# Window attention on one core: the row scores' stationary operand cut from 128 to 100 columns, and the odd half of the result combined in one instruction

## The chip, the cores and the metric

The kernel runs on one core of a Trainium2 chip. The metric is the device time of one execution in microseconds (us). A core has five engines with a queue of instructions each: TensorE (PE in the profile; its weight loads are listed apart as PEld), VectorE (DVE), ScalarE (ACT), GpSimd (POOL) and SyncE (SP), which issues the DMAs here. They work side by side and wait for each other through semaphores. TensorE's clock has two levels, 1.2 and 2.4 GHz; the profile gives the granted clock as a share of the upper one.

## The reference

The input `x` is 4 images of 128 channels and 112x112 pixels. It is group-normalised, goes through a windowed self-attention, and is added to the result:

```python
xs = jnp.roll(x, (-SHIFT, -SHIFT), axis=(-2, -1))            # SHIFT = 3
qkv = jnp.einsum('bchw,oc->bohw', xs, w_qkv) + b_qkv[None, :, None, None]
# 7x7 windows: 49 tokens each; 8 heads of 16 channels
scores = jnp.einsum('bxyhqd,bxyhkd->bxyhqk', q, k) * scale
attn = jax.nn.softmax(scores, axis=-1)
out = jnp.einsum('bxyhqk,bxyhkd->bxyhqd', attn, v)
# windows put back in place, rolled back
x = x + _L0_conv_ref(_gn(x), L0_conv_w_qkv, L0_conv_b_qkv)
```

## The kernel before

There are 4 x 16 x 16 windows of 49 tokens. The unit of work is a group of 8 windows (half a band of windows), so there are 128 groups. A group of 392 tokens goes through a software pipeline that is some four groups deep: in one step every engine works at different stages of groups g-3 to g+2, in an order that is written out by hand in a `step` function of each engine. Two steps stand in the body of a loop on each engine, and only semaphores tie the engines together.

TensorE's step is: `sum_keys` and `weigh` of group g-2, `project_v` of g, `turn_max` and `column_scores` (half 0) of g-1, `row_scores` (half 0) of g, `spread_inverse` of g-2, `project_k` of g+1, `column_scores` (half 1) of g-1, `row_scores` (half 1) of g, `project_q` of g+1. Products in which precision matters are computed with operands split into a high and a low float16 part, three matmuls for one product.

Heads come in pairs. Each pair has 32 channels, so it lies on a strip of 32 partitions, and the four strips hold the eight heads. `q_masks` holds, for each window, 100 columns: 49 queries and a zero with the channels of the even head kept, then 49 queries and a zero with those of the odd head kept. The scores are made twice. `row_scores` (L730) has queries on the partitions and keys along the columns, and exists only so that VectorE can take the maximum over the keys (`maximum`, L573). `column_scores` (L747, L756) has keys on the partitions, in two blocks of 64 rows for two windows, and feeds the exponential.

In `row_scores` the stationary operand is `q_masks[rows, ...]`, 32 partitions by 128 columns from the start of a window's 100, so that 28 columns of the next window (or of padding) are computed and never read; the moving operand is 49 columns of `k_hi` or `k_lo`. Each call makes 8 windows x 3 products x 2 head pairs, 48 matmuls. The two head pairs of a product stand on different strips of 32 partitions and write different banks, so they run side by side: a call is 24 such pairs of matmuls, each matmul with its own weight load. There are two calls in a group, 256 in all, and 12288 matmuls. `maximum` already reads only `psum[0:ROWS2]`, with ROWS2 = 100.

`weigh` (L794) multiplies the values by the probabilities into the two `OUT_BANKS`, one bank for each of the two windows of a pair of windows, at columns `a*100` for pair a of 4. Of each 100 columns, 49 belong to the even and 49 (from column 50) to the odd head. `evac_even` on ScalarE (L390) scales the even part into `even_out`, `join` on VectorE (L592) adds the scaled odd part, with one instruction for each bank, into `summed`, whose windows stand in their own order. `spread_inverse` (L806) spreads the inverse sums of the softmax, one matmul of 49 columns for each window, and `scale_rows` (L599) multiplies them with `summed` into `mixed`, which GpSimd adds to the image (L305).

Of the kernel before, what the change touches and what calls it, by code (L numbers as in the profile page):

```python
# [6 lines left out]
B, C, H, W = 4, 128, 112, 112  # L7
# [4 lines left out]
TOK = WS * WS  # L12
BANDS = H // WS
NW = W // WS
GW = NW // 2
GT = GW * TOK
HP = HEADS // 2
PC = 2 * HD
QP = TOK + 1
ROWS2 = 2 * QP  # L20
PITCH = 64
PAIRS = GW // 2
# [13 lines left out]
def window_attention(nc, x, w_qkv, b_qkv, out):  # L36
    f32, f16, bf16, i32 = mybir.dt.float32, mybir.dt.float16, mybir.dt.bfloat16, mybir.dt.int32
    ALU, ACT, AX = mybir.AluOpType, mybir.ActivationFunctionType, mybir.AxisListType
# [5 lines left out]
    with ctx:  # L44
        def sb(name, shape, dt=f32):
            return ctx.enter_context(nc.sbuf_tensor(name, shape, dt))

        def sem(name):
            return ctx.enter_context(nc.semaphore(name))
# [7 lines left out]
        q_masks = sb("q_masks", [C, 2, 2 * Q_LEN + Q_PAD], f16)  # L57
# [6 lines left out]
        inv_hi, inv_rows = sb("inv_hi", [C, TOK], f16), sb("inv_rows", [C, TOK], f16)  # L64
        even_out = sb("even_out", [C, 2, PAIRS, TOK])
        summed = sb("summed", [C, GW, TOK])
        mixed = sb("mixed", [C, 2, GW, TOK])
# [17 lines left out]
        pick_head = sb("pick_head", [C, GW, C], f16)  # L85
# [7 lines left out]
        v_scale = sb("v_scale", [C, 2])  # L93
# [11 lines left out]
        psum = ctx.enter_context(nc.psum_tensor("psum", [128, 8, 512], f32))  # L105
        ROW_BANKS, COL_BANKS, OUT_BANKS = slice(0, 2), slice(2, 4), slice(6, 8)
        NEG_BANK, SUM_BANK, QK_BANK, V_BANK, INV_BANK = 0, 3, 4, 5, 5
        SPARE_SUM = slice(PAIRS * ROWS2, PAIRS * ROWS2 + TOK)
        SPARE = slice(PAIRS * ROWS2, (PAIRS + 1) * ROWS2)

# [21 lines left out]
        even_done, join_done, mixed_done, add_done = (sem(n) for n in ("even_done", "join_done", "mixed_done", "add_done"))  # L132

        def wait(engine, semaphore, count):

            if not isinstance(count, int) or count > 0:
                engine.wait_ge(semaphore, count)  # L140
# [188 lines left out]
        def _(act):  # L329
# [56 lines left out]
            def evac_even(g):  # L386
                act.wait_ge(out_mm, g + 1)
                wait(act, join_done, g + 1)
                even = psum[:, OUT_BANKS, 0:PAIRS * ROWS2].rearrange("p s (a e q) -> p s a e q", e=2, q=QP)[:, :, :, 0, 0:TOK]
                nc.scalar.activation(even_out[:, :, :, :], even, ACT.Identity, scale=v_scale[:, 0:1]).then_inc(even_done, 1)  # L390

            def step(g, n, par):
                if live(g):
                    evac_q(g)
                if live(g + 2):
                    normalise(g + 2, n + 1, par)
                if live(g - 2):
                    evac_even(g - 2)
                    high_inverse(g - 2)
                if live(g - 1):  # L400
                    evac_neg(g - 1)
                if live(g):
                    evac_v(g, par)
                if live(g - 1):
                    exp(g - 1, 0)
                if live(g + 1):
                    evac_k(g + 1)
                if live(g - 1):
                    exp(g - 1, 1)
# [18 lines left out]
        def _(dve):  # L428
# [147 lines left out]
            def invert(g):  # L576
                dve.wait_ge(sum_mm, g + 1)
                nc.vector.reciprocal(inv32[:, :], psum[:, SUM_BANK, SPARE_SUM]).then_inc(inv_done, 1)

# [6 lines left out]
            def join(g):  # L586
                dve.wait_ge(even_done, g + 1)
                wait(dve, mixed_done, g + 1)
                by_side = summed[:, :, :].rearrange("p (a s) q -> p s a q", s=2)
                for s in range(2):  # L590
                    odd = psum[:, OUT_BANKS.start + s, 0:PAIRS * ROWS2].rearrange("p (a e q) -> p a e q", e=2, q=QP)[:, :, 1, 0:TOK]
                    last = nc.vector.scalar_tensor_tensor(by_side[:, s], odd, v_scale[:, 1:2], even_out[:, s, :, :], ALU.mult, ALU.add)  # L592
                last.then_inc(join_done, 1)

            def scale_rows(g, par):
                dve.wait_ge(inv_mm, g + 1)
                dve.wait_ge(join_done, g + 2)
                wait(dve, add_done, g - 1)
                nc.vector.tensor_tensor(mixed[:, par, :, :].rearrange("p w q -> p (w q)"), psum[:, INV_BANK, 0:GT],  # L599
                                        summed[:, :, :].rearrange("p w q -> p (w q)"), ALU.mult).then_inc(mixed_done, 1)  # L600

            def step(g, n, par, chunks=(), image_at=None, first=None, before=None, after=None):


                if first:
                    first()
                if live(g):
                    low_q(g)
                if live(g - 2):
                    invert(g - 2)  # L610
                if live(g):
                    mask_q(g, par)
                if live(g - 2):
                    low_inverse(g - 2)
                    join(g - 2)
                if before:
                    before()
                if live(g):
                    maximum(g, par, 0)
                for chunk in chunks:  # L620
                    take_stats(image_at + chunk * STAT, chunk)
                if after:
                    after()
                if live(g - 2):
                    scale_rows(g - 2, par)
                if live(g):
                    maximum(g, par, 1)
# [50 lines left out]
        def _(pe):  # L678
# [3 lines left out]
            for j in range(3):  # L682
                last = nc.tensor.transpose(psum[:, QK_BANK, j * C:(j + 1) * C], w_nat[:, j, :], ident[:, :])
# [36 lines left out]
            def row_scores(g, par, j):  # L720

                if j == 0:
                    pe.wait_ge(q_masked, g + 1)
                    pe.wait_ge(k_split, g + 1)
                wait(pe, max_done[1 - j], g + j)
                for w in range(GW):
                    for n, (low, k) in enumerate(((0, k_hi), (0, k_lo), (Q_LEN, k_hi))):
                        for h in (2 * j, 2 * j + 1):
                            rows = slice(h * PC, (h + 1) * PC)
                            last = nc.tensor.matmul(psum[:, ROW_BANKS.start + h - 2 * j, w * TOK:(w + 1) * TOK],  # L730
                                                    q_masks[rows, par, low + w * ROWS2:low + w * ROWS2 + 128], k[rows, par, w, 0:TOK],
                                                    start=n == 0, stop=n == 2, skip_group_check=True)
                last.then_inc(row_mm[j], 1)

# [39 lines left out]
            def sum_keys(g):  # L774
                pe.wait_ge(exp_done[0], g + 1)
                pe.wait_ge(exp_done[1], g + 1)
                for a in range(PAIRS):
                    for e in range(2):
                        for c in range(HP):
                            last = nc.tensor.matmul(psum[c * PC:(c + 1) * PC, SUM_BANK, SPARE_SUM],  # L780
                                                    sum_rows[:, a, e, :, :, :].rearrange("p t w s -> p (t w s)"),
# [4 lines left out]
            def weigh(g, par):  # L786
                pe.wait_ge(v_evac, g + 1)
                wait(pe, join_done, g + 1)
                pe.sem_inc(waited_pe, 1)
                for a in range(PAIRS):  # L790
                    for c in range(HP):
                        for s in range(2):
                            side = slice(PITCH * s, PITCH * (s + 1))
                            last = nc.tensor.matmul(psum[c * PC:(c + 1) * PC, OUT_BANKS.start + s, a * ROWS2:(a + 1) * ROWS2],  # L794
                                                    v_rows[side, par, a, c * PC:(c + 1) * PC], probs_t[side, c, a, :],
                                                    start=True, stop=True, skip_group_check=True)
                last.then_inc(out_mm, 1)

            def spread_inverse(g, after_v=True):
                pe.wait_ge(inv_split, g + 1)  # L800
                if after_v:
                    pe.wait_ge(v_evac, g + 3)
                else:
                    pe.wait_ge(mixed_done, g + 1)
                for w in range(GW):
                    last = nc.tensor.matmul(psum[:, INV_BANK, w * TOK:(w + 1) * TOK], pick_head[:, w, :], inv_rows[:, :],  # L806
                                            start=True, stop=True, skip_group_check=True)
                last.then_inc(inv_mm, 1)

# [51 lines left out]
```

## Time and profile before

| | |
|---|---|
| time, median of 3 runs | 1022.41 us (1020.85 to 1024.33) |
| the profiled execution's own time | 1024.01 us |
| its span, first to last instruction | 1022.1 us |
| mean granted clock of TensorE | 0.985 |
| matmuls and weight loads | 46595 each |
| of them row scores (L730) | 12288 each |

The span is the stretch that the trace covers; 1.9 us of the execution's own time lie around it. A row of the timeline merges neighbouring instructions of one form: its start, its length to the end of the last of them, and their count after the x. A matmul's duration in the trace, some 0.2 us, is that of its passage through the array, and many are under way at once; what a matmul costs when many follow one another is the distance from one start to the next, called the step below. The duration of a weight load is its passage too.

### The profile page before, as it was taken

How to read it: one execution, taken by the hardware profiler on the slowest of the kernel's cores; microseconds unless marked ns; L12 is line 12 of the kernel's file. 1: busy time of each engine (PE TensorE's matmuls, PEld its weight loads, DVE VectorE, ACT ScalarE, POOL GpSimd, SP SyncE). 2: the span in 40 equal slices, each digit the busy share in tenths (PEclk: the TensorE clock that was granted, in tenths of full speed). 3: DMA queues.
4: the chain of work that ended last, by engine and by line, in shares of the span. 5: the costliest groups of instructions: out<-in, count | busy, mean ns of one | idle time of the engine just before them, and what ended most of it. 6: DMA issues, size and time to landing. Idle time of an engine off the chain costs nothing. (4 is left out here: it accounts for less than half of the span.)

```text
span 1022.1 us, 104511 instructions
## 1 busy us (share of the span) xinstructions
PE 967.7 (95%) x46595; PEld 764.0 (75%) x46595; DVE 793.8 (78%) x1532; ACT 696.6 (68%) x1297; POOL 596.4 (58%) x1067
## 2 busy tenths in 40 slices
PE   0589999999999999999999999999999999999985
PEld 0367777777778777777778787777778777777764
DVE  6667888888888888888888888888877777777762
ACT  1447777777777777777777777777777777777752
POOL 1345665666666566666656665666666566666641
PEclk9979999999999999999999999999999999999995
DMA  9301101111111111111111000000000000000000
GB/s 381 131 4 63 63 31 63 63 49 45 63 63 33 61 63 57 37 63 63 40 55 47 32 16 31 31 31 16 32 31 16 31 31 31 16 31 31 19 31 35
DMA packets 29920, 51.96 MB, mean 51 GB/s; under 512 B 3650, under 2 KB 28868, under 8 KB 29764
## 3 DMA queue, kind: packets, MB, share of 16 engines
q1 hardware_dynamic: 29892, 51.59, 14.3%
q8 instruction: 17, 0.28, 0.1%
q14 instruction: 11, 0.09, 0.0%
HBM read 25.89 MB, written 25.69 MB: 50 GB/s over the span
## 5 line engine op out<-in xcount | busy, mean ns | idle before, releaser
L573 DVE TENSOR_REDUCE neg_max<-psum 100x16 f32<-100x784 f32 x256 | 249.4, 974 | 159.8 <-PE psum L730 159.8
L373 ACT ACTIVATE probs_t<-psum,exp_scale 128x800 f32<-128x800 f32 x256 | 237.3, 927 | 82.1 <-PE psum L747 52.8
L283 POOL TENSOR_SCALAR k_hi<-k 128x392 f16<-128x392 f32 x128 | 67.8, 530 | 230.2 <-PE psum L747 228.1
L730 PE MATMUL psum<-k_hi,q_masks 32*128 32x49 f16 x8192 | 197.5, 179 | 1.1 <-issue 0.6
L747 PE MATMUL psum<-q_masks,k_hi 32*64 32x100 f16 x8192 | 187.7, 207 | 3.3 <-issue 3.3
L305 POOL TENSOR_TENSOR stage<-mixed,image 128x343 f32 (+7 forms) x256 | 160.9, 650 | 43.5 <-issue 32.3
L730 PEld LDWEIGHTS psum<-k_hi,q_masks 32*128 32x128 f16 x8192 | 174.9, 91 | 10.9 <-issue 0.7
L730 PE MATMUL psum<-k_lo,q_masks 32*128 32x49 f16 x4096 | 182.2, 179 | 0.0
L566 DVE TENSOR_SCALAR q_masks<-q_halves,even_odd 128x800 f16<-128x800 f16 x256 | 171.6, 710 | 0.1
L747 PEld LDWEIGHTS psum<-q_masks,k_hi 32*64 32x64 f16 x8192 | 151.6, 105 | 26.4 <-issue 4.1
L730 PEld LDWEIGHTS psum<-k_lo,q_masks 32*128 32x128 f16 x4096 | 160.6, 91 | 0.0
L747 PE MATMUL psum<-q_masks,k_lo 32*64 32x100 f16 x4096 | 158.4, 204 | 0.0
L350 ACT ACTIVATE xn<-image,shift_c,rstd_c 128x21 f32 (+6 forms) x256 | 131.3, 564 | 8.0 <-DVE shift_c L553 6.1
L780 PEld LDWEIGHTS psum<-probs_t,sum_rows 128*32 128x32 f32 x8192 | 101.3, 111 | 45.2 <-issue 45.1
L794 PE MATMUL psum<-probs_t,v_rows 64*32 64x100 f32 x8192 | 132.0, 254 | 2.2 <-issue 2.2
L285 POOL TENSOR_TENSOR k_lo<-k,k_hi 128x392 f16<-128x392 f32 x128 | 117.2, 916 | 10.7
L275 POOL TENSOR_TENSOR xn_lo<-xn,xn_hi 128x392 f16<-128x392 f32 x128 | 116.4, 909 | 10.7
L780 PE MATMUL psum<-probs_t,sum_rows 128*32 128x49 f32 x8192 | 119.0, 210 | 2.3 <-issue 1.2
L357 ACT ACTIVATE k<-psum,k_bias 128x392 f32<-128x392 f32 x128 | 75.3, 588 | 64.6 <-PE psum L697 64.6
L747 PEld LDWEIGHTS psum<-q_masks,k_lo 32*64 32x64 f16 x4096 | 118.6, 106 | 0.0
L362 ACT ACTIVATE q_halves<-psum,q_bias 128x392 f16<-128x392 f32 x128 | 75.8, 592 | 52.6 <-PE psum L703 52.6
L794 PEld LDWEIGHTS psum<-probs_t,v_rows 64*32 64x32 f32 x8192 | 103.2, 106 | 11.2 <-issue 2.6
(120 smaller groups left out, 1881.8 us busy)
## 6 DMA issues: line engine op xcount, KB each, us to landing
out_dram<-stage SPq DMA_DIRECT2D x64, 224.0 KB, 2.0
out_dram<-stage SPq DMA_DIRECT2D x64, 168.0 KB, 1.9
image<-in_x_dram SPq DMA_DIRECT2D x32, 224.0 KB, 2.6
image<-in_x_dram SPq DMA_DIRECT2D x1, 6104.0 KB, 27.3
image<-in_x_dram SPq DMA_DIRECT2D x34, 168.0 KB, 2.5
image<-in_x_dram SPq DMA_DIRECT2D x6, 896.0 KB, 9.7
image<-in_x_dram SPq DMA_DIRECT2D x1, 728.0 KB, 14.1
w_nat<-in_L_conv_w_qkv_dram SPq DMA_DIRECT2D x1, 192.0 KB, 2.4
```

The costliest lines, as they stand in the source:

```text
L275: nc.gpsimd.tensor_tensor(xn_lo[:, par, :, 0:TOK], xn[:, :, :], xn_hi[:, par, :, 0:TOK], ALU.subtract).then_inc(x_split, 1)
L285: nc.gpsimd.tensor_tensor(k_lo[:, par, :, 0:TOK], k, k_hi[:, par, :, 0:TOK], ALU.subtract).then_inc(k_split, 1)
L305: last = nc.gpsimd.tensor_tensor(pixel_view(stage[:, bass.ds(st, BAND)], piece), token_view(mixed[:, half, :, :], piece), pixel_view(image ...
L350: last = nc.scalar.activation(token_view(xn, piece), pixel_view(image[:, bass.ds(at, BAND)], piece), ACT.Identity, bias=shift_c[:, 0:1], s ...
L362: nc.scalar.activation(q_halves[:, 0, :, 0:TOK], psum[:, QK_BANK, 0:GT].rearrange("p (w q) -> p w q", q=TOK), ACT.Identity, bias=q_bias[:, ...
L373: nc.scalar.activation(probs_t[:, 2 * u:2 * u + 2, :, :].rearrange("p h a q -> p h (a q)"), psum[:, COL_BANKS, 0:PAIRS * ROWS2], ACT.Exp, ...
L566: last = nc.vector.tensor_scalar(both[:, :, e, :], q_halves[:, :, :, :].rearrange("p l w q -> p (l w) q"), even_odd[:, e:e + 1], None, ALU ...
L573: nc.vector.tensor_reduce(neg_max[:, par, 2 * j:2 * j + 2, :], psum[0:ROWS2, ROW_BANKS, 0:GT] .rearrange("p h (w k) -> p h w k", k=TOK), A ...
L730: last = nc.tensor.matmul(psum[:, ROW_BANKS.start + h - 2 * j, w * TOK:(w + 1) * TOK], q_masks[rows, par, low + w * ROWS2:low + w * ROWS2 ...
L747: last = nc.tensor.matmul(psum[side, COL_BANKS.start + h % 2, a * ROWS2:(a + 1) * ROWS2], k[rows, par, w, :], q_masks[rows, par, low + w * ...
L780: last = nc.tensor.matmul(psum[c * PC:(c + 1) * PC, SUM_BANK, SPARE_SUM], sum_rows[:, a, e, :, :, :].rearrange("p t w s -> p (t w s)"), pr ...
L794: last = nc.tensor.matmul(psum[c * PC:(c + 1) * PC, OUT_BANKS.start + s, a * ROWS2:(a + 1) * ROWS2], v_rows[side, par, a, c * PC:(c + 1) * ...
```

## The change

The row scores' stationary operand becomes the 100 columns of one window, and their result 100 partitions. The results of `weigh` are put at columns `a*128` in place of `a*100`, so that the two banks can be read as one run of eight slots at equal distances; `join` then takes the odd parts of all eight windows in one instruction. `summed` is kept in the order bank, pair; `spread_inverse` puts its windows in that order too (`PLACE`), and `scale_rows` reads both in it and writes `mixed` in the windows' own order.

```diff
+        PLACE = [w // 2 + PAIRS * (w % 2) for w in range(GW)]
...
-                even = psum[:, OUT_BANKS, 0:PAIRS * ROWS2].rearrange("p s (a e q) -> p s a e q", e=2, q=QP)[:, :, :, 0, 0:TOK]
+                even = psum[:, OUT_BANKS, :].rearrange("p s (a q) -> p s a q", a=PAIRS)[:, :, :, 0:TOK]
...
-                by_side = summed[:, :, :].rearrange("p (a s) q -> p s a q", s=2)
-                for s in range(2):
-                    odd = psum[:, OUT_BANKS.start + s, 0:PAIRS * ROWS2].rearrange("p (a e q) -> p a e q", e=2, q=QP)[:, :, 1, 0:TOK]
-                    last = nc.vector.scalar_tensor_tensor(by_side[:, s], odd, v_scale[:, 1:2], even_out[:, s, :, :], ALU.mult, ALU.add)
+                odd = psum[:, OUT_BANKS, :].rearrange("p s (a q) -> p (s a) q", a=PAIRS)[:, :, QP:QP + TOK]
+                last = nc.vector.scalar_tensor_tensor(summed[:, :, :], odd, v_scale[:, 1:2], even_out[:, :, :, :].rearrange("p s a q -> p (s a) q"),
+                                                      ALU.mult, ALU.add)
...
-                nc.vector.tensor_tensor(mixed[:, par, :, :].rearrange("p w q -> p (w q)"), psum[:, INV_BANK, 0:GT],
-                                        summed[:, :, :].rearrange("p w q -> p (w q)"), ALU.mult).then_inc(mixed_done, 1)
+                nc.vector.tensor_tensor(mixed[:, par, :, :].rearrange("p (a s) q -> p s a q", s=2),
+                                        psum[:, INV_BANK, 0:GT].rearrange("p (s a q) -> p s a q", s=2, q=TOK),
+                                        summed[:, :, :].rearrange("p (s a) q -> p s a q", s=2), ALU.mult).then_inc(mixed_done, 1)
...
-                            last = nc.tensor.matmul(psum[:, ROW_BANKS.start + h - 2 * j, w * TOK:(w + 1) * TOK],
-                                                    q_masks[rows, par, low + w * ROWS2:low + w * ROWS2 + 128], k[rows, par, w, 0:TOK],
+                            last = nc.tensor.matmul(psum[0:ROWS2, ROW_BANKS.start + h - 2 * j, w * TOK:(w + 1) * TOK],
+                                                    q_masks[rows, par, low + w * ROWS2:low + (w + 1) * ROWS2], k[rows, par, w, 0:TOK],
...
-                            last = nc.tensor.matmul(psum[c * PC:(c + 1) * PC, OUT_BANKS.start + s, a * ROWS2:(a + 1) * ROWS2],
+                            last = nc.tensor.matmul(psum[c * PC:(c + 1) * PC, OUT_BANKS.start + s, a * C:a * C + ROWS2],
...
-                    last = nc.tensor.matmul(psum[:, INV_BANK, w * TOK:(w + 1) * TOK], pick_head[:, w, :], inv_rows[:, :],
+                    last = nc.tensor.matmul(psum[:, INV_BANK, PLACE[w] * TOK:(PLACE[w] + 1) * TOK], pick_head[:, w, :], inv_rows[:, :],
```

## Rows read from the trace of the kernel before

**Rows 1.** The page, parts 1 and 2: busy time by engine, and TensorE's granted clock.

```profile
PE 967.7 (95%) x46595; PEld 764.0 (75%) x46595; DVE 793.8 (78%) x1532; ACT 696.6 (68%) x1297; POOL 596.4 (58%) x1067
PEclk9979999999999999999999999999999999999995
```

**Rows 2.** Busy time by stretch: stretch, length, each engine's busy time, granted clock, DMA.

```profile
60.00:980.00 920.00, 919.24 (x44842) 727.79 (x44841) 740.58 (x1395) 664.51 (x1233) 568.56 (x983) 0.99 0.12 41
```

**Rows 3.** Timeline, TensorE's matmuls within one period: start, length, line, operation, shapes, count.

```profile
501.92 0.35 PE L756 MATMUL psum<-neg_rows,pick_window 32*128 32x100 bf16 x8
502.11 0.18 PE L730 MATMUL psum<-k_hi,q_masks 32*128 32x49 f16 x2
502.14 0.18 PE L730 MATMUL psum<-k_lo,q_masks 32*128 32x49 f16 x2
...
502.69 0.18 PE L730 MATMUL psum<-k_hi,q_masks 32*128 32x49 f16 x2
502.80 0.37 PE L806 MATMUL psum<-inv_rows,pick_head 128*128 128x49 f16 x8
...
503.97 0.21 PE L747 MATMUL psum<-q_masks,k_lo 32*64 32x100 f16 x4
...
504.41 0.21 PE L747 MATMUL psum<-q_masks,k_hi 32*64 32x100 f16 x4
504.56 0.20 PE L730 MATMUL psum<-k_hi,q_masks 32*128 32x49 f16 x2
```

**Rows 4.** Lines L730, L747, L715, L683: weight loads, minimum/median/maximum in ns, first and last start.

```profile
L730 PEld LDWEIGHTS psum<-k_hi,q_masks x8192: 90/91/118, 41.1 to 1001.5; 32*128 32x128 f16 x200
...
L747 PEld LDWEIGHTS psum<-q_masks,k_hi x8192: 101/105/170, 46.8 to 1009.9; 32*64 32x64 f16 x200
...
L715 PEld LDWEIGHTS psum<-w_hi,xn_hi x512: 97/98/151, 38.8 to 994.4; 128*128 128x128 f16 x171
...
L683 PEld LDWEIGHTS psum<-ident,w_nat x3: 183/226/229, 3.8 to 4.1; 128*128 128x128 f32 x3
```

**Rows 5.** Timeline, weight loads of L715 near the start of the run.

```profile
39.30 0.15 PEld L715 LDWEIGHTS psum<-w_lo,xn_hi 128*128 128x128 f16 x1
...
40.26 0.15 PEld L715 LDWEIGHTS psum<-w_lo,xn_hi 128*128 128x128 f16 x1
```

**Rows 6.** Timeline, matmuls of L715 in mid-run.

```profile
500.46 0.22 PE L715 MATMUL psum<-w_hi,xn_hi 128*128 128x128 f16 x1
...
501.07 0.22 PE L715 MATMUL psum<-w_lo,xn_hi 128*128 128x128 f16 x1
```

**Rows 7.** Groups by line: busy us, mean ns, and idle time before them with its releaser.

```profile
L573 DVE TENSOR_REDUCE neg_max<-psum 100x16 f32<-100x784 f32 x256 | 249.4, 974 | 159.8 <-PE psum L730 159.8
...
L592 DVE SCALAR_TENSOR_TENSOR summed<-psum,v_scale,even_out 128x196 f32<-128x196 f32 x256 | 94.4, 407 | 0.0
L558 DVE SCALAR_TENSOR_TENSOR q_halves<-psum,q_bias,q_halves 128x392 f16<-128x392 f32 x128 | 80.4, 628 | 35.4 <-ACT q_halves L362 35.1
L599 DVE TENSOR_TENSOR mixed<-psum,summed 128x392 f32<-128x392 f32 x128 | 70.7, 552 | 1.0 <-PE psum L806 0.6
```

**Rows 8.** Timeline, VectorE, from one second maximum to the next; idle time before in brackets.

```profile
505.75 0.96 DVE L573 TENSOR_REDUCE neg_max<-psum 100x16 f32<-100x784 f32 x1
...
507.60 1.33 DVE L566 TENSOR_SCALAR q_masks<-q_halves,even_odd 128x800 f16<-128x800 f16 x2
...
509.04 0.74 DVE L592 SCALAR_TENSOR_TENSOR summed<-psum,v_scale,even_out 128x196 f32<-128x196 f32 x2
510.34 0.97 DVE L573 TENSOR_REDUCE neg_max<-psum 100x16 f32<-100x784 f32 x1 [0.57 <-PE psum L730]
511.23 0.62 DVE L493 BATCH_NORM_STATS2 stats<-image 128x6 f32<-128x448 f32 x1
511.76 0.55 DVE L599 TENSOR_TENSOR mixed<-psum,summed 128x392 f32<-128x392 f32 x1
512.79 0.97 DVE L573 TENSOR_REDUCE neg_max<-psum 100x16 f32<-100x784 f32 x1 [0.48 <-PE psum L730]
```

## The prediction

> **What bounds the kernel now.** I read the page's busy times first: TensorE is busy 95% of the span, VectorE 78%, ScalarE 68% [rows 1]. A busy matmul row is not yet a full engine, so the next view is the busy time by stretch. Between 60 and 980 us TensorE is without a matmul under way for 0.76 us of 920 [rows 2], while VectorE idles for 179. The third view is the timeline of one period. What the reader should look for in it is a gap before a stage of TensorE, and there is none longer than a change of stage: the row scores' last pair starts at 502.69 and the next stage at 502.80; the column scores' last four start at 504.41 and the row scores at 504.56, which is one step of 44 ns and 0.1 us for the switch [rows 3]. The last view is who waits for whom. VectorE idles before the maximum for 159.8 us in all, and all of that is for L730 [rows 7]. So TensorE is the bound in every stage, and one more nanosecond in a matmul stage is one more nanosecond in the period. The chain that ended last covers only the tail behind the last group, so I don't use it.
>
> **The row scores.** From the pair at 502.14 (the second of the call) to the last at 502.69 there are 22 steps, so a step is 0.55/22 = 25.0 ns [rows 3]. What sets it? The moving operand has 49 columns, 20.4 ns at 2.4 GHz, so it isn't the stream alone. The weight load is 128 columns on each strip. At one column per cycle that would be 53 ns, over twice the step, so a load of 128 columns must go faster than one column per cycle. The rows on the loads say the same. A load of 128 float16 columns takes 91 ns, one of 64 columns on the same 32 partitions takes 105 [rows 4]: half the columns, 14 ns more. The large f32 load of 128 columns at the start took 226 ns (median), against 151 at most for the float16 load of the same tile, 75 ns more [rows 4]. Near the start TensorE runs at its lower level: nine steps of L715 take 0.96 us, 107 ns for 128 columns, which is 1.2 GHz; in mid-run eleven take 0.61 us, 55 ns, which is 2.4 GHz [rows 5, 6]. The clock row of the page says 9 in that early slice [rows 1], so I go by the steps there. I take the f32 load at 4 us to have run at the lower level too. If it is a load at one column per cycle, 107 ns, the fast one takes 107 - 75 = 32 ns, that is 38 cycles for 128 columns. So there are two forms of load: a fast one, of 128 float16 columns, and a plain one, which the loads of 64 have. The question on which the change hangs is which of the two 100 columns get.
>
> I take the plain form. The only row of fewer than 128 float16 columns, L747's, has it, and nothing in the trace shows a fast load of any other width than 128. A plain load of 100 columns is then 100/2.4 = 41.7 ns, longer than the stream of 20.4 and than the step of 25.0. Loads run beside the stream before them: the column scores load 64 columns (26.7 ns plain) and stream 100 (41.7 ns) in a step of 0.44/10 = 44.0 ns from 503.97 to 504.41 [rows 3], less than the 68 of both in turn. So the longer of load and stream counts, with 2.3 ns for the change from one to the next, which is what that step has over 41.7. The new step is 41.7 + 2.3 = 44.0 ns, 19.0 more than now. The trace bounds this load from both sides. It is not below 29 ns: the 75 ns more for 128 columns at the lower level are 37.5 at the upper, and 100/128 of that is 29. It is not above 69 ns if a plain load's time goes with its columns, since 64 of them fit into 44.0. I take 41.7, since it is what one column per cycle gives, and the row of L747 (14 ns more than the fast load; (64 - 38)/2.4 = 11 by this reckoning) is nearest to it.
>
> The Trainium skill, TensorE: Matmul & The Clock Gate, section "Weight-path perf modes", says that the fast weight load is on only when the number of weights is 128 and the type is not FP32. It agrees with the rows on 128, 64 and f32; on 100 columns it speaks against this change, and with it the sum would be as above.
>
> The sum: a call has 24 pairs of matmuls and thus 23 steps between them, and the step after the last is the stream, as now. 23 x 19.0 = 437 ns a call, x 256 calls = 111.9 us. The first load of a call is 41.7 - 16 = 26 ns longer. In the first half it follows a stage of the same tile (32*128), and its load can go ahead under the stream before; in the second half it follows the switch from 32*64 [rows 3], and is exposed: 128 x 26 ns = 3.3 us. (Neither exposed: 0; both: 6.7.) Together +115.2 us.
>
> **The rest.** Three edits are on other engines or only move data. (a) `join`: two instructions of 407 ns, 0.74 us from start to end [rows 7, 8], become one of 392 columns. The nearest row is L558, the same operation from PSUM with 392 columns, 628 ns [rows 7]. VectorE gets 0.11 us a group, 14 us in all. They count nothing, as behind `join` VectorE already waits 0.57 us for the row scores [rows 8]; in the other direction the same 0.57 covers it. (b) `scale_rows` reads and writes runs of 49 in place of one run: 552 ns now, and up to the 628 of L558 [rows 7]. A gain is excluded, as the elements are as many and only the runs are shorter. The 0.08 us are covered by the 0.48 us of idle time before the second maximum [rows 8]. Without that cover it would be 128 x 0.08 = 10 us. (c) `evac_even`, `weigh` and `spread_inverse` have the same count of instructions, columns and runs at other addresses: nothing. No wait is added, no instruction passes another, and SP's and POOL's queues are as they were. What is late next? The distance from the end of each call to the engines' answer stays. After the second maximum (505.75) VectorE has the masks of q ready at 508.93; the maximum at 510.34 waited for a call that needs them and lasts some 0.8 us (502.11 to 502.87), so it began at about 509.5, 0.6 us after the masks [rows 3, 8]. TensorE's stages in between are unchanged, and so is this slack. After the first call (maximum at 510.34) VectorE has a longer call in front of the second maximum than now. So no slack shrinks, and TensorE stays the bound.
>
> **Sum.** The profiled execution took 1024.0 us; 1024.0 + 115.2 = 1139.2. It lies 1.6 above the median of the runs, so against that 1022.4 + 115.2 = 1137.6, about 1138 us.
>
> **Rivals.** (1) The fast load stays on for 100 columns. For it: the loads of 64 columns stand in a tile of 64 columns (32*64) and the 128s in a tile of 128, so that the rows can't tell whether the width or the tile makes the slow load [rows 4], and the new load keeps the tile of 128. Against it: no row shows it. It decides as soon as the load is below the step of 25 ns. Then TensorE's step stays, the 14 us saved on VectorE are covered, and the time is 1022, not slower. The Trainium skill, TensorEngine Tiling (Array Packing), "Restrictions", says that column tiling switches the fast weight load off, which would explain the 64s in this way. (2) A plain load does not run beside the stream on its own strip. For it: with two strips in use nothing else is there to fill the time. Against it: the column scores' 44.0 ns [rows 3], and 25.0 now, below 16 + 20.4. The step would be 41.7 + 20.4 = 62.1, so 37.1 x 23 x 256 = 218 us and 3 more: 1244. (3) The loads of the two strips go one after the other when they are plain and across the whole width: step 83.3, so 58.3 x 5888 = 343 and 3 more: 1369. Against it: the column scores have two strips and two halves in a step, and already the two strips in turn, 53 ns, would not fit into 44.0 [rows 3]; but those are other tiles. The Trainium skill, TensorE: Matmul & The Clock Gate, section "LDWEIGHTS", gives columns/1.2 ns for a load, 83 for 100 columns, by which the step would be 83 too; it gives 53 for 64 columns, which the step of 44.0 contradicts. (4) A plain load faster than one column per cycle: 29 ns, step 31.3, 6.3 x 5888 = 37 us: 1060 to 1120.
>
> **Chances.** Forecast 0.66 (1120 to 1155: a step of 41.7 with no first load exposed gives 98 us, one of 46.5 with both exposed 133); fast load kept 0.10; load and stream in turn or a part of it (1155 to 1250) 0.10; strips in turn 0.08; faster plain load 0.05; anything with a gain 0.01. The range takes in the forecast, the slower end of it to (2), and the near part of (4): 1105 to 1250, with about 0.8 in it. About 0.3% is what a measurement of this kernel can tell from no change. Slower by more than that: 0.66 + 0.10 + 0.08 + 0.05 = 0.89. Within it: 0.09 of the case of the fast load; its last 0.01 and the 0.01 of other gains make 0.02 for faster.
>
> **What would show it.** In the profile after: L730's weight loads 32x100, at 105 + 36/2.4 = 120 ns in place of 91 (91 or less if rival 1 holds); pairs of L730 44 ns apart, a call of 1.05 us in place of 0.6; a period longer by 0.9 us; TensorE still without gaps, VectorE's wait for L730 grown from 159.8 to some 275 us; `summed` x128 near 628 ns. The prediction is wrong if the load is 100 columns in under 105 ns, if the step isn't the longer of load and stream, or if the granted clock falls in mid-run because the array now streams for less than half of the time in these stages.

## The result and the profile after

The changed kernel takes 1147.7 us (median of 4 runs, 1145.2 to 1150.2), the kernel before beside it 1021.6 us (1019.0 to 1024.3). The ratio is 1.123, 95% interval 1.119 to 1.128: slower by 126 us. The profiled execution took 1148.8 us.

The page of the changed kernel, parts 1 and 2, for [rows 1], and below it the busy time by stretch for [rows 2]:

```profile
PE 1097.7 (96%) x46595; PEld 896.9 (78%) x46595; DVE 778.5 (68%) x1404; ACT 697.2 (61%) x1297; POOL 596.6 (52%) x1067
...
PEclk9989999999999999999999999999999999999996
```

```profile
60.00:1100.00 1040.00, 1039.45 (x44636) 850.96 (x44630) 723.15 (x1267) 661.71 (x1225) 566.63 (x980) 1.00 0.11 36
```

The instructions of TensorE are as many as before, and it still has no gap: 0.55 us of 1040 without a matmul under way. The other engines have the same work in a longer span. The granted clock is as before, so the time went into TensorE's instructions themselves. The weight loads of the row scores (L731 in the changed kernel), minimum/median/maximum in ns, for the first of [rows 4]:

```profile
L731 PEld LDWEIGHTS psum<-k_hi,q_masks x8192: 116/122/203, 40.5 to 1128.4; 32*100 32x100 f16 x200
```

A load of 100 columns takes 122 ns where that of 128 took 91. TensorE's timeline around both calls of a group, for [rows 3]:

```profile
502.66 0.35 PE L757 MATMUL psum<-neg_rows,pick_window 32*128 32x100 bf16 x8
502.85 0.19 PE L731 MATMUL psum<-k_hi,q_masks 32*100 32x49 f16 x2
502.88 0.20 PE L731 MATMUL psum<-k_lo,q_masks 32*100 32x49 f16 x2
...
503.90 0.20 PE L731 MATMUL psum<-k_hi,q_masks 32*100 32x49 f16 x2
504.04 0.37 PE L807 MATMUL psum<-inv_rows,pick_head 128*128 128x49 f16 x8
...
505.65 0.21 PE L748 MATMUL psum<-q_masks,k_hi 32*64 32x100 f16 x4
505.79 0.23 PE L731 MATMUL psum<-k_hi,q_masks 32*100 32x49 f16 x2
505.86 0.20 PE L731 MATMUL psum<-k_lo,q_masks 32*100 32x49 f16 x2
...
506.88 0.20 PE L731 MATMUL psum<-k_hi,q_masks 32*100 32x49 f16 x2
507.02 0.34 PE L704 MATMUL psum<-xn_hi,w_hi 128*128 128x392 f16 x1
```

The reader should count from the second pair to the last, 22 steps: 1.02 us in either call, so a step is 46.4 ns instead of 25.0. (Starts are printed to 0.01 us, so a step taken over 22 is good to half a nanosecond.) A second call of the kernel before, its first two pairs, its last and the stage behind it, for which [rows 3] has only the first pair:

```profile
511.98 0.20 PE L730 MATMUL psum<-k_hi,q_masks 32*128 32x49 f16 x2
512.02 0.18 PE L730 MATMUL psum<-k_lo,q_masks 32*128 32x49 f16 x2
...
512.57 0.18 PE L730 MATMUL psum<-k_hi,q_masks 32*128 32x49 f16 x2
512.68 0.34 PE L703 MATMUL psum<-xn_hi,w_hi 128*128 128x392 f16 x1
```

And the first pair of the first call one group later, before and after:

```profile
509.54 0.18 PE L730 MATMUL psum<-k_hi,q_masks 32*128 32x49 f16 x2
...
511.30 0.19 PE L731 MATMUL psum<-k_hi,q_masks 32*100 32x49 f16 x2
```

From 502.11 [rows 3] to 509.54 a group takes 7.43 us; from 502.85 to 511.30 it takes 8.45, which is 1.02 more. The weight loads of the first pair in either call of the changed kernel:

```profile
502.81 0.12 PEld L731 LDWEIGHTS psum<-k_hi,q_masks 32*100 32x100 f16 x2
...
505.79 0.12 PEld L731 LDWEIGHTS psum<-k_hi,q_masks 32*100 32x100 f16 x2
```

VectorE's groups, for [rows 7]:

```profile
L574 DVE TENSOR_REDUCE neg_max<-psum 100x16 f32<-100x784 f32 x256 | 249.6, 975 | 303.2 <-PE psum L731 303.0
...
L591 DVE SCALAR_TENSOR_TENSOR summed<-psum,v_scale,even_out 128x392 f32<-128x392 f32 x128 | 78.6, 614 | 0.0
L599 DVE TENSOR_TENSOR mixed<-psum,summed 128x392 f32<-128x392 f32 x128 | 70.8, 553 | 0.7 <-PE psum L807 0.3
```

`join` is one instruction of 614 ns, `scale_rows` costs what it did, and VectorE waits 303 us for the row scores where it waited 160.

### The profile page after: what moved, and what is told of

The parts are those of the page before. It is cut to its first block, busy times and chain, and to the rows that moved or that the text cites. A ratio compares the mean times of both kernels' runs of the same rounds, so it can differ in the third digit from the quotient of the medians.

```text
span 1146.9 us, 104383 instructions
## 1 busy us (share of the span) xinstructions
PE 1097.7 (96%) x46595; PEld 896.9 (78%) x46595; DVE 778.5 (68%) x1404; ACT 697.2 (61%) x1297; POOL 596.6 (52%) x1067
## 3 DMA queue, kind: packets, MB, share of 16 engines
q1 hardware_dynamic: 29892, 51.59, 12.7%
## 4 chain that ended last, share of the span: by engine, by line
PE 95%; DVE 2%; issue 1%; ACT 0%; POOL 0%; DMA 0%; ACTq 0%; SPq 0%; POOLq 0%; DVEq 0%
PE psum L731 26%; PE psum L748 15%; PE psum L795 11%; PE psum L781 10%; PE psum L716 7%; PE psum L704 7%; PE psum L757 6%; PE psum L698 6%; PE psum L712 4%; PE psum L807 3%; DVE stats L494 1%; PE psum L738 1%; DMA bias<-in_L_conv_b_qkv_dram 0%; ACT xn L351 0%; ACT probs_t L374 0%
## 5 line engine op out<-in xcount | busy, mean ns | idle before, releaser
L731 PE MATMUL psum<-k_hi,q_masks 32*100 32x49 f16 x8192 | 331.4, 201 | 0.4 <-DVE q_masks L567 0.4
L731 PEld LDWEIGHTS psum<-k_hi,q_masks 32*100 32x100 f16 x8192 | 309.8, 123 | 10.2 <-DVE q_masks L567 0.7
L731 PE MATMUL psum<-k_lo,q_masks 32*100 32x49 f16 x4096 | 306.5, 201 | 0.0
L731 PEld LDWEIGHTS psum<-k_lo,q_masks 32*100 32x100 f16 x4096 | 259.1, 123 | 0.0
```

Source lines behind the costliest of these rows:

```text
L731: last = nc.tensor.matmul(psum[0:ROWS2, ROW_BANKS.start + h - 2 * j, w * TOK:(w + 1) * TOK], q_masks[rows, par, low + w * ROWS2:low + (w + ...
```

## The experiments

The theory: a load of 100 columns goes at one column per cycle, is longer than the stream of 49 columns beside it, and so sets the step of the row scores (L730; L731 in the changed kernel); all else in the change is hidden. Its rivals: another part of the change has a share in the loss; the new step is a fixed cost of an odd width; load and stream take turns. Each ratio below is against runs of the kernel before on the same chip.

**The two parts, each alone.** `rows100_only` is the kernel before with

```diff
-... psum[:, ROW_BANKS.start + h - 2 * j, ...], q_masks[rows, par, low + w * ROWS2:low + w * ROWS2 + 128]
+... psum[0:100, ROW_BANKS.start + h - 2 * j, ...], q_masks[rows, par, low + w * ROWS2:low + w * ROWS2 + 100]
```

> The kernel before with the row scores' edit alone. Theory (the plain weight load of 100 columns sets the step): step of L730 46.4 ns as in the changed kernel, weight load 122 ns, 23 x 21.4 ns x 256 calls = 126 us more: 1148 us, the whole loss. Rival (part of the loss comes from the new places of the results or the joined instruction): less than that, say 1100 us.

1150.8 us, ratio 1.127 (1.124 to 1.130). The interval overlaps that of the whole change, and the load's median is 122 ns again.

`join_only` is the changed kernel with the same two slices at 128.

> The changed kernel with the row scores' stationary operand at 128 columns again. Theory: TensorE is the bound and the 0.12 us that VectorE saves in a group fall into its wait for the row scores: 1022 us, within 0.3%, step of L730 25.0 ns. Rival (VectorE's time counts): 128 x 0.12 = 15 us less, 1007; or the runs of 49 cost something: slower by up to 10 us.

1020.8 us, ratio 1.0007 (0.9994 to 1.0021). Two of VectorE's groups in its trace, with the columns of [rows 7]:

```profile
L574 DVE TENSOR_REDUCE neg_max<-psum 100x16 f32<-100x784 f32 x256 | 249.4, 974 | 173.8 <-PE psum L731 173.4
...
L591 DVE SCALAR_TENSOR_TENSOR summed<-psum,v_scale,even_out 128x392 f32<-128x392 f32 x128 | 78.4, 612 | 0.0
```

`join` became one instruction of 612 ns, and VectorE's wait for TensorE grew from 159.8 us [rows 7] to 173.4, by 14 us, which is the 0.11 us a group that the start-to-end times gave. So the whole loss is the row scores', and the joined instruction brings nothing and costs nothing.

**The width.** `rows112_only` and `rows127_only` are the kernel before with 112 and 127 in place of the 100 above.

> The kernel before with a stationary operand of 112 columns in the row scores. Theory (a plain load of one column per cycle at 2.4 GHz plus 4.7 ns): step 46.7 + 4.7 = 51.4 ns, 26.4 x 5888 = 155 us more: 1178 us, slower than with 100. Rival A (the fast load holds for widths that are a multiple of 16 or 32, or near 128): 1022 us. Rival B (the step of 46.4 is a fixed cost of a load that isn't 128 wide, and its width counts nothing): 1148 us.

> The kernel before with a stationary operand of 127 columns in the row scores, one less than before. Theory (fast load only at exactly 128, else one column per cycle): step 52.9 + 4.7 = 57.6 ns, 32.6 x 5888 = 192 us more: 1215 us, the slowest of all. Rival (the cost grows smoothly as the width leaves 128): near 1022 us.

With 112 columns 1182.3 us, ratio 1.158 (1.155 to 1.161); with 127 columns 1296.0 us, ratio 1.269 (1.265 to 1.273). The load, and the second and the last pair of a call, of 112 columns:

```profile
L730 PEld LDWEIGHTS psum<-k_hi,q_masks x8192: 121/127/212, 40.1 to 1159.9; 32*112 32x112 f16 x200
```

```profile
502.08 0.21 PE L730 MATMUL psum<-k_lo,q_masks 32*112 32x49 f16 x2
...
503.22 0.21 PE L730 MATMUL psum<-k_hi,q_masks 32*112 32x49 f16 x2
```

and of 127 columns, with the clock row of its page:

```profile
L730 PEld LDWEIGHTS psum<-k_hi,q_masks x8192: 128/135/228, 40.2 to 1275.6; 32*127 32x127 f16 x200
```

```profile
502.06 0.22 PE L730 MATMUL psum<-k_lo,q_masks 32*127 32x49 f16 x2
...
503.36 0.22 PE L730 MATMUL psum<-k_hi,q_masks 32*127 32x49 f16 x2
```

```profile
PEclk9998898999989999899989999899998999989986
```

| columns | load, median ns | step, ns | time, us |
|---|---|---|---|
| 128 | 91 | 25.0 | 1019.5 |
| 127 | 135 | 1.30/22 = 59.1 | 1296.0 |
| 112 | 127 | 1.14/22 = 51.8 | 1182.3 |
| 100 | 122 | 1.02/22 = 46.4 | 1150.8 |

One column less than 128 costs 34 ns a step, and from there the step falls as the operand gets narrower, 12.7 ns over 27 columns (0.47 a column; one cycle at 2.4 GHz is 0.42). So neither a fixed cost nor a gradual one: a fast load at 128, at all three other widths a plain one whose time goes with its columns. The 127 were 81 us over what was expected. The step explains (59.1 - 57.6) x 5888 = 9 us of that. For the rest the mean granted clock is what differs, 0.928 in place of 0.985: a share of 2 x 0.072 = 14% of the time at the lower level in place of 3%; 11% of 1296 us is 143 us, half of which would be saved at the upper level, 71 us. This is an estimate from the two means, and it covers the 72 us that are left.

**Load beside stream.** `rows100_keys25` is the changed kernel, `rows128_keys25` the kernel before, each with 24 of the 49 keys left out of the row scores and of their maximum:

```diff
-    psum[..., w * TOK:(w + 1) * TOK], q_masks[...], k[rows, par, w, 0:TOK]
+    psum[..., w * 25:(w + 1) * 25], q_masks[...], k[rows, par, w, 0:25]
...
-    psum[0:ROWS2, ROW_BANKS, 0:GT].rearrange("p h (w k) -> p h w k", k=TOK)
+    psum[0:ROWS2, ROW_BANKS, 0:GW * 25].rearrange("p h (w k) -> p h w k", k=25)
```

> The changed kernel, with the row scores of the first 25 keys of each window only (moving operand 25 columns, and the maximum over 25 in place of 49; keys 25 to 48 are left out of the maximum alone). Theory (the load of 100 columns alone sets the step and hides the stream): step stays 46.4 ns, 1149 us, as the changed kernel. Rival (load and stream take turns in part, so that the stream's columns count): 24 columns less are 10 ns, step 36.4, 59 us less: 1090 us. The share in between tells how much of the stream is exposed. If the granted clock falls, as it did with 127 columns (0.928), the steps tell and the time doesn't.

> The kernel before with the row scores of 25 keys in place of 49, as in the run beside it. It tells what sets the 25.0 ns of before. If the stream and a fixed 4.7 ns: step 15.1 but for the fast load, 16 + 4.7 = 20.7, so 25 us less: 997 us. If a fixed least distance of such pairs sets it: step 25.0, 1020 us. If the fast load sets it: 25.0 too, and then a fast load would take some 20 to 25 ns and not 16.

`rows100_keys25` took 1249.7 us, ratio 1.227 (1.225 to 1.230), 100 us more than with 49 keys, and neither account had said that. The time tells nothing of load and stream, because the clock fell: its mean is 0.891. The steps do. Here are the first, second and last pair of one call and the first pair one group later, then part of a call 11 us after the first (L731), and the busy time of TensorE in three stretches, with the granted clock behind it:

```profile
505.06 0.18 PE L731 MATMUL psum<-k_hi,q_masks 32*100 32x25 f16 x2
505.09 0.20 PE L731 MATMUL psum<-k_lo,q_masks 32*100 32x25 f16 x2
...
506.12 0.19 PE L731 MATMUL psum<-k_hi,q_masks 32*100 32x25 f16 x2
...
513.49 0.18 PE L731 MATMUL psum<-k_hi,q_masks 32*100 32x25 f16 x2
...
516.93 0.24 PE L731 MATMUL psum<-k_lo,q_masks 32*100 32x25 f16 x2
...
518.32 0.24 PE L731 MATMUL psum<-k_hi,q_masks 32*100 32x25 f16 x2
```

```profile
500.00:508.00 8.00, 8.00 (x356) 1.00 0.26 87
508.00:516.00 8.00, 8.00 (x344) 1.00 0.04 13
516.00:524.00 8.00, 8.00 (x240) 0.57 0.13 47
```

At a granted clock of 1.00, 22 steps take 1.03 us: 46.8 ns, as with 49 keys (46.4). Half of the stream's columns are gone and no step is shorter, so the load alone sets it. A group takes 8.43 us (505.06 to 513.49) where the changed kernel takes 8.45, so at the upper clock this kernel is no slower than that one, and the 100 us lie in the stretches at the lower clock. In the third stretch 16 steps take 1.39 us: 86.9 ns, where 100 columns at 1.2 GHz are 83.3. The step goes with TensorE's clock: a column a cycle, and 3 to 5 ns more.

`rows128_keys25` took 1017.5 us, ratio 0.9988 (0.9977 to 0.9999). Its second and last pair of a call:

```profile
506.95 0.17 PE L730 MATMUL psum<-k_lo,q_masks 32*128 32x25 f16 x2
...
507.50 0.17 PE L730 MATMUL psum<-k_hi,q_masks 32*128 32x25 f16 x2
```

22 steps in 0.55 us, 25.0 ns: the step of before isn't the stream either. Whether it is a least distance between such pairs or the fast load itself these runs don't tell. The Trainium skill, TensorE: Matmul & The Clock Gate, section "Wait — 56ns, not 53.3ns?", states that start-to-start never drops below about 25 ns however few the columns. The trace agrees, with 49 and with 25 columns, if the pair is taken as one. But a pair is two matmuls on two strips, 12.5 ns for each, so for the single matmul the measurement decides against the sentence.

**A narrow load under a long stream.** `v_width113` makes the same cut at another place of the kernel before: `project_v`, whose moving operand has 128 columns.

```diff
-    nc.tensor.matmul(psum[:, V_BANK, a * C:(a + 1) * C], xs[...].rearrange("p w k -> p (w k)"), ...)
+    nc.tensor.matmul(psum[0:113, V_BANK, a * C:(a + 1) * C], xs[...].rearrange("p w k -> p (w k)")[:, 0:113], ...)
```

> The kernel before with another stationary operand cut from 128 to the columns in use: that of project_v (L715), 113 columns in place of 128 (49, 15 of padding, 49), 12 matmuls in a group over the whole array, with a moving operand of 128 columns. Theory (a plain load costs only what it is longer than the stream beside it): the load goes from 98 to some 128 ns in the trace, 113/2.4 + 4.7 = 51.8 ns is less than the step of 55.5, so the steps stay 55 to 56 ns and the time 1020 us. Rival (any load but one of 128 costs, in part beside the stream and in part in turn with it): load and stream in turn would give 100 ns a step, 45 x 12 x 128 = 69 us more, 1089 us; the same 21 ns as in the row scores 32 us more, 1052 us.

1021.1 us, ratio 1.000 (0.998 to 1.002). Its loads, and the second and the last matmul of a group's twelve:

```profile
L715 PEld LDWEIGHTS psum<-w_hi,xn_hi x512: 129/132/221, 37.6 to 991.4; 128*113 128x113 f16 x171
```

```profile
505.06 0.22 PE L715 MATMUL psum<-w_hi,xn_lo 128*113 128x128 f16 x1
...
505.62 0.22 PE L715 MATMUL psum<-w_lo,xn_hi 128*113 128x128 f16 x1
```

The load is the plain one, 132 ns in place of 98, but ten steps take 0.56 us, 56 ns as before [rows 6]. The same kind of edit, which cost 21 ns a step in the row scores, costs nothing where the stream (53 ns) is longer than the load (47); at 21 ns a step it would have been 32 us here.

**A change of tile.** At the stages' borders [rows 3] 0.1 us pass between one matmul's start and the next beyond the step. The row of matmuls shows no gap there, since the earlier ones are still under way. `one_switch_less` is the kernel before with the two parts of the second column scores in the other order:

```diff
-                    less_maximum(u, True)
-                    last = scores_of_keys(g, par, u, False)
+                    scores_of_keys(g, par, u, True)
+                    last = less_maximum(u, False)
```

> The kernel before, with the second half of the column scores in the order of the first: scores of the keys first, then the maximum's matmuls (L757 after L748). The stages of TensorE then meet at one change of tile less in a group: 128*128 to 32*64 to 32*128 in place of 128*128 to 32*128 to 32*64 to 32*128. Theory (TensorE is the bound in all stages and a change of tile costs 0.09 to 0.1 us on it): 128 x 0.1 = 12 us less, 1008 us. Rival (the gap is a wait for ScalarE's exponential, which moves along): 1020 us.

> The same order together with the changed kernel's joined instruction, row scores at 128 columns. Theory: as one_switch_less, 1008 us, since VectorE's 14 us stay covered. Rival (with TensorE faster, VectorE's time begins to count): some us below one_switch_less.

`one_switch_less` took 1006.8 us, ratio 0.990 (0.987 to 0.993), and `join_one_switch_less` 1005.9 us, ratio 0.988 (0.986 to 0.990). Both beat the kernel before; between them there is no difference that these runs can tell. The timeline of `one_switch_less` from `project_k` to the second row scores, and what the weight loads waited for:

```profile
500.41 0.33 PE L697 MATMUL psum<-xn_hi,w_lo 128*128 128x392 f16 x1
500.67 0.24 PE L747 MATMUL psum<-q_masks,k_hi 32*64 32x100 f16 x4
...
501.18 0.21 PE L747 MATMUL psum<-q_masks,k_hi 32*64 32x100 f16 x4
501.33 0.35 PE L756 MATMUL psum<-neg_rows,pick_window 32*128 32x100 bf16 x8
501.51 0.18 PE L730 MATMUL psum<-k_hi,q_masks 32*128 32x49 f16 x2
```

```profile
PEld psum L747 <- ACT probs_t L373: 41.2, 124, 0.3
```

L756's eight matmuls are four steps of 44 ns, 0.18 us, and the row scores follow right on them: the same tile, no gap. 12.5 us in 128 groups are 0.1 us for the change that is gone. The wait for the exponential (0.33 us each time) is still there. It is one of the weight loads' row alone, in which the matmuls of `project_k` are still streaming, and so it isn't a stop of TensorE.

## Why the prediction was right

The time was forecast at 1138 us and came out at 1147.7; the mechanism was the one forecast. How near the number came is in part luck: four smaller terms were off and partly cancelled.

- **What bounds the kernel.** Right: a group is 1.02 us longer on TensorE, which over 128 groups is 131 us, and 126 of them came out in the time. What VectorE saved did not come out at all (`join_only`).
- **Which form of load.** Right. This was the step on which all hung, and it was argued from rows that could not tell width from tile. The widths 100, 112, 113 and 127 settle it, since none of them fits a tile of 64 columns: only 128 was fast. Rival 1, that the fast load stays on in a tile that isn't narrowed to 64, falls with them. Whether the loads of 64 (L747) are plain for their width or for their tile stays open. The rule of the Trainium skill, TensorE: Matmul & The Clock Gate, section "Weight-path perf modes", that 128 columns are needed, is borne out down to the one column between 127 and 128.
- **Load beside stream, longer one counts.** Right, against rivals 2 and 3: 62 and 83 ns a step were never seen at the upper clock, and neither taking away half of the stream (`rows100_keys25`) nor a plain load under a longer stream (`v_width113`) changed a step. Rival 4, a plain load of 29 ns, falls with the 46.4.
- **The size of the step.** This term was too small: 44.0 was forecast, 46.4 measured. The 41.7 ns of one column per cycle fit, but the 2.3 ns between one and the next came from a stage that is bound by its stream; where the load is the bound it is 4.7 ns (5.1 with 112 columns, 6.2 with 127). Over the 44 steps in a group that are not the first of a call, 2.4 x 44 x 128 = 14 us more than forecast.
- **The first load of a call.** Right in its kind: in the first call the load goes ahead of its matmul, in the second, behind the change of tile, it doesn't (loads at 502.81 and 505.79, their matmuls at 502.85 and 505.79). In size the term was too large. The sum had 19 ns for the first step of either call and 26 more for the second call, 64 in all. In the first call that step is 30 ns now (502.85 to 502.88) and was 30 before (502.11 to 502.14 [rows 3]); in the second it is 70 (505.79 to 505.86) and was 40 (511.98 to 512.02). That is 30 ns in place of 64, 4 us less than forecast.
- **The step behind the last pair.** Put at nothing ("the stream, as now"), and wrong. It was 0.11 us to the next stage (502.69 to 502.80 [rows 3], 512.57 to 512.68) and is 0.14 in both calls (503.90 to 504.04, 506.88 to 507.02). A group is 1.02 us longer, and its calls, from first to last pair, 0.47 and 0.50 (1.05 for 0.58, 1.09 for 0.59), which leaves 0.05 us for this, 6 us in all. What makes the step longer these runs don't show.
- **Start and end of the run.** Not in the sum. Together the terms above give 115 + 14 - 4 + 6 = 131 us, the 1.02 us of a group times 128, but the time grew by 126. Between the first and the last load of the row scores lie 127.5 us more than before (41.1 to 1001.5 [rows 4], 40.5 to 1128.4 now), and behind the last load, to the end of the span, 2 fewer (20.6 and 18.5). So the groups at the start and at the end grew by some 5 us less in all; what sets their time was not looked into. Without this luck the miss would have been 15 us and not 10.
- **The rest at nothing.** Right: 614 ns for the joined instruction (628 forecast), 553 for `scale_rows` (552 to 628 forecast).
- **VectorE's wait.** Forecast at some 275 us, measured 303. The sum had left out that VectorE's own 14 us fall into this wait as well; the other 14 are the longer group (131 us in place of 115).
- **The clock.** Named as what would make the prediction wrong, and given no price. It stayed at 0.989 in the changed kernel, so what was feared for it did not happen there; but it fell to 0.928 with 127 columns and to 0.891 with 100 columns and 25 keys. The forecast had no term for it, and in kernels as near as these it was worth 70 to 100 us.

## What to carry to other kernels

What a narrower stationary operand is worth is read from the step, not from the columns saved: with 100 to 127 float16 columns the load went at a column a cycle, and that is free only as long as the stream beside it is longer (113 columns under 128: nothing; 100 under 49: 21 ns a matmul pair, 12% of this kernel). The 28 unused columns were what kept the load fast, so they are best left in. Where TensorE has no gaps, an instruction saved on another engine was worth nothing, while the order of stages is worth a look: one change of tile less in each group gave 1%.

## What the runs showed of the hardware that was not expected

TensorE's granted clock fell although its row of matmuls has no gap. In `rows100_keys25` matmuls were under way for all of the 8 us from 516 to 524, and the granted clock there is 0.57, with steps as at 1.2 GHz; just before, at a granted 1.00, the array streamed 25 columns in steps of 46.8 ns. It is the kernel with fewer columns to stream, and it is 100 us slower than the one with 49. `rows128_keys25` streams 25 columns too, but in steps of 25.0 ns, and its mean is 0.986. On what exactly the fall depends was not tried.

Idle time in the weight loads' row need not be a stop of TensorE (the 0.33 us before L747 above). And the busy share of that row rose from 75% to 78% while the kernel became 12% slower; the matmuls' steps told where the time went.
